# DLRM tower on one core: sixteen selected fields (two of them gathered in the middle units) and a 512- or 1024-word fill behind each gather, against twenty selected fields everywhere and three one-word fills

## The chip, the core and the metric

One NeuronCore of a Trainium2 chip runs the whole program. The time is device microseconds of one execution. Compute engines are PE (TensorE), DVE (VectorE), ACT (ScalarE) and POOL (GpSimd); SP (SyncE) only issues DMAs.

## The reference

2048 samples have 32 categorical fields each. Every field has a table with rows of 64 floats (26 tables have 1000 or 1250 rows, three 12500 and three 125000).

```python
e = jnp.stack([tbl_0[ids[:, 0]], ..., tbl_31[ids[:, 31]]], axis=1)   # 2048 x 32 x 64
gram = jnp.einsum('bnd,bmd->bnm', e, e)
z = gram[:, rows, cols]                       # 496 pairs, upper triangle
h = jnp.concatenate([z, dense_ctx], axis=1)   # 2048 x 512
h = jnp.maximum(h @ W_top1 + b_top1, 0.0)     # 512 -> 512
h = jnp.maximum(h @ W_top2 + b_top2, 0.0)     # 512 -> 256
y = h @ W_top3                                # 256 -> 1
```

All in float32.

## The kernel before, in words

The batch is cut into four units of 512 samples (`UNITS`, `UNIT`), and the samples of a unit into two rounds of 256 (`r`). A unit goes through four stages: its 32 embedding vectors per sample are fetched and laid into `vecs` (64 dims on partitions, twice, 256 samples x 32 fields on the free axis); the gram matrices are formed on PE from `vecs`; they go out to a DRAM scratch (`products`) and come back in another layout as `z`; the three layers of the tower run on `z`. The tower of a unit is woven into the gram stage of the next one, and that of the last unit stands alone at the end.

Fields are fetched in two ways.

*Selected* fields have small tables (1000 or 1250 rows, that is 8 or 10 chunks of 125 rows). The table lies in SBUF as three bfloat16 parts (`tabs`, PARTS = 3) whose sum is the float32 value; they are made in unit 0, on the way. Packed float32 chunks come by DMA into one of four stage slots (`load_stage`, SP). ACT copies the high part (`high`, L317), DVE subtracts it (`rest`, L436), ACT copies the middle part (`middle`, L322), DVE subtracts again (`low`, L441). For each chunk of 125 rows and 512 samples DVE makes a one-hot block (L453, `tensor_scalar` with `is_equal`, float16 ids broadcast to 128 partitions in `ids_wide`, 128x512), and PE multiplies each part of the chunk by it (L498, three matmuls for one one-hot). Fields go in pairs: one of a pair fills partitions 0 to 63 of `sel_ps`, the other 64 to 127. A pair is worked off in two halves, each of 4 or 5 chunks of both fields. `onehot` is a ring of four pieces (`RING`), a piece being one half of one field, so DVE can be two halves ahead of PE: it waits on `onehot_used` for the piece four back. PE waits on `onehot_ready` before each half. ACT empties `sel_ps` into `vecs` with four copies (L329, `selected`); there are two buffers.

*Gathered* fields come by indirect DMA from the tables in DRAM, issued by POOL (`gather`, L296): 128 rows of 256 bytes in one, so two (h) for each field and round. Behind each gather POOL fills a piece of `spare` with zeros (L303), a tile that nothing reads. Before the fill it waits until the fill before is done (`spaced`). The fill has 1024 words a partition in unit 0 and 512 in the others (`SPACING`). POOL then waits for nothing but `gat_full`: the slots in `rows` of a unit can be written over once PE has transposed those of the unit before. PE turns four fields at a time (`turn`, L513, four transposes into `gat_ps`, or two in the fifth turn of units 1 and 2), ACT copies them into `vecs` (`gathered`, L337).

Sixteen fields are selected in units 0 and 3 (eight pairs, 132 chunks: fourteen fields of 8 chunks and two of 10). In units 1 and 2 (`SHIFTED`) the last pair (fields 30 and 31, 10 chunks each) is gathered as well, which leaves seven pairs (112 chunks) and makes eighteen gathered fields.

The order of work is written by hand, one list for each engine. On PE a unit is: `select` of pairs 2 and up, with the turns of round 0 behind pairs 4, 5, ...; the turns that are left; layer 1 of the unit before in four pieces, each followed by a quarter of the gram matmuls of round 0 (L528); the turns of round 1, with `select` of pairs 0 and 1 of the next unit between them; layer 2, gram of round 1 and layer 3. ACT and DVE follow the same order. DVE in unit 0 does `one_hots`, `low`, `one_hots`, `rest` by turns, one pair after the other. ACT in unit 0 does `selected(g)`, `high(g+4)`, `middle(g+4)`. The gram stage of a unit starts when all its `selected` and `gathered` copies of round 0 are done.

SP issues all other DMAs in one list: the stage loads, `ids_wide` for each pair of the next unit (`load_wide`, each once DVE is done with the same pair of the unit before), then `products` out and `z` back.

## Time and profile before

| | |
|---|---|
| median of 3 runs | 574.52 us (572.3 to 587.05) |
| the profiled execution, its own time | 577.56 us |
| its span | 575.8 us |
| PE busy | 403.8 us (70%) |
| POOL busy | 465.0 us (81%) |
| DVE busy | 292.7 us (51%) |
| ACT busy | 141.8 us (25%) |
| granted TensorE clock, mean | 0.852 |

The span runs from the first to the last instruction of the profiled execution; 1.8 us of its own time lie around it. The granted clock is given as a share of full speed: 1.00 is 2.4 GHz, 0.50 is 1.2 GHz. The chain is the work that ended last, followed back from the end: what stands in it set the time. An instruction's duration in the trace runs from its start to its end, and consecutive ones of one engine overlap, so the pace is to be read from starts, or from the time of several divided by their count.

### The profile page before, as it was taken

The numbers are of one execution on the slowest core, as the hardware profiler recorded it, in microseconds if no ns is written. First come the engines' busy times: TensorE is split into PE (matmuls) and PEld (weight loads), VectorE is DVE, ScalarE is ACT, GpSimd is POOL, SyncE is SP. The second block draws the span as 40 slices with busy tenths as digits, with TensorE's granted clock in tenths as the row PEclk, the third lists the DMA queues.
The fourth block names the chain that finished last, engine by engine and source line by source line (L and its number), as shares of the span: only waits on it lengthen the run. The fifth ranks groups of instructions, "written<-read, shape, count | busy, mean of one in ns | idle before, by whom it ended". The sixth has DMA issues, their size and how long they took to land.

```text
span 575.8 us, 13498 instructions
## 1 busy us (share of the span) xinstructions
PE 403.8 (70%) x5956; PEld 217.7 (38%) x5956; DVE 292.7 (51%) x513; ACT 141.8 (25%) x232; POOL 465.0 (81%) x552
## 2 busy tenths in 40 slices
PE   0556554756874678787975687868966788799877
PEld 0222222323543334334432344334432344445655
DVE  4999999999180299300810499100900599100000
ACT  5002233422200334310201434111110434212212
POOL 7999999999998899989998999889988999950000
PEclk9977778787695699888986799887996799989989
DMA  8414311110111475110111584101011651003340
GB/s 271 140 51 141 98 33 32 30 35 15 21 21 23 73 166 150 29 23 20 22 21 23 101 190 124 23 21 21 21 23 23 132 119 19 19 16 64 72 83 1
DMA packets 39060, 36.11 MB, mean 63 GB/s; under 512 B 14869, under 2 KB 27991, under 8 KB 38874
## 3 DMA queue, kind: packets, MB, share of 16 engines
q1 hardware_dynamic: 29866, 25.14, 18.0%
q0 software_dynamic: 8704, 8.93, 7.6%
q8 instruction: 47, 0.77, 0.5%
q10 hardware_dynamic: 432, 1.18, 0.5%
q14 instruction: 11, 0.09, 0.0%
HBM read 27.15 MB, written 8.07 MB: 61 GB/s over the span
## 4 chain that ended last, share of the span: by engine, by line
PE 42%; DVE 39%; issue 11%; ACT 4%; DMA 2%; SPq 2%; ACTq 0%; DVEq 0%
DVE onehot L453 35%; PE gram_ps L528 14%; PE tower_ps L542 11%; PE sel_ps L498 9%; PE tower_ps L551 5%; ACT vecs L329 2%; PE tower_ps L560 2%; DVE work L436 2%; DVE tabs L441 2%; PE gat_ps L513 2%; DMA work<-in_packed_dram 1%; ACT work L346 1%; SPq L207 1%; DMA products<-work 1%; SPq L209 1%
## 5 line engine op out<-in xcount | busy, mean ns | idle before, releaser
L453 DVE TENSOR_SCALAR onehot<-ids_wide,row_ids 128x512 bf16<-128x512 f16 x488 | 269.4, 627 | 113.2 <-PE sel_ps L498 113.2
L296 POOL DMA_INDIRECT rows<-in_tbl_dram,gat_ids x272 | 287.0, 1055 | 46.3 <-issue 44.3
L498 PE MATMUL sel_ps<-onehot,tabs 128*64 128x512 bf16 x1464 | 200.4, 433 | 98.1 <-DVE onehot L453 79.5
L303 POOL MEMSET spare<- 128x512 f32 (+1 forms) x272 | 177.9, 654 | 0.1
L498 PEld LDWEIGHTS sel_ps<-onehot,tabs 128*64 128x64 bf16 x1464 | 95.9, 123 | 196.8 <-issue 95.2
L528 PE MATMUL gram_ps<-vecs 64*32 64x32 f32 x4096 | 71.2, 214 | 61.4 <-issue 48.8
L329 ACT COPY vecs<-sel_ps 64x256 f32<-64x256 f32 x120 | 71.9, 599 | 123.1 <-PE sel_ps L498 70.2
L528 PEld LDWEIGHTS gram_ps<-vecs 64*32 64x32 f32 x4096 | 54.6, 115 | 93.7 <-issue 80.5
L542 PE MATMUL tower_ps<-work,w_sb 128*128 128x512 f32 (+1 forms) x160 | 73.8, 622 | 2.8 <-DMA work<-products 2.8
L460 DVE COPY work<-gram_ps 128x512 f32<-128x512 f32 x8 | 5.2, 687 | 127.9 <-PE gram_ps L528 127.9
L542 PEld LDWEIGHTS tower_ps<-work,w_sb 128*128 128x128 f32 x160 | 35.7, 230 | 31.4 <-issue 25.3
L352 ACT ACTIVATE h<-tower_ps,b_sb 128x512 f32<-128x512 f32 (+1 forms) x20 | 12.0, 602 | 81.2 <-PE tower_ps L542 81.2
L551 PE MATMUL tower_ps<-h,w_sb 128*128 128x512 f32 (+1 forms) x80 | 31.0, 537 | 1.1 <-ACT h L352 1.1
L337 ACT COPY vecs<-gat_ps 128x512 f32<-128x512 f32 (+1 forms) x36 | 19.5, 570 | 34.8 <-PE gat_ps L513 29.5
L346 ACT COPY work<-gram_ps 128x512 f32<-128x512 f32 x24 | 13.0, 588 | 59.3 <-PE gram_ps L528 59.3
L322 ACT CAST tabs<-work 128x1024 bf16<-128x1024 f32 (+1 forms) x8 | 8.6, 1072 | 70.0 <-DVE work L436 70.0
L513 PE MATMUL gat_ps<-ident,rows 128*128 128x128 f32 x136 | 21.7, 293 | 4.9 <-ACT vecs L337 4.9
L513 PEld LDWEIGHTS gat_ps<-ident,rows 128*128 128x128 f32 x136 | 15.1, 145 | 14.4 <-issue 8.6
L551 PEld LDWEIGHTS tower_ps<-h,w_sb 128*128 128x128 f32 x80 | 15.1, 197 | 12.5 <-issue 9.7
L359 ACT ACTIVATE h<-tower_ps,b_sb 128x512 f32<-128x512 f32 (+1 forms) x10 | 5.5, 598 | 36.3 <-PE tower_ps L551 36.3
L560 PE MATMUL tower_ps<-h,w_sb 128*1 128x512 f32 (+1 forms) x20 | 11.1, 689 | 1.9 <-ACT h L359 1.9
L436 DVE TENSOR_TENSOR work<-work,tabs 128x1024 f32<-128x1024 f32 (+1 forms) x8 | 10.0, 1248 | 4.2 <-ACT tabs L317 4.2
(13 smaller groups left out, 25.1 us busy)
## 6 DMA issues: line engine op xcount, KB each, us to landing
ids_wide<-ids_scratch SPq DMA_DIRECT2D x30, 256.0 KB
rows<-in_tbl_dram,gat_ids POOLq DMA_INDIRECT x272
products<-work SPq DMA_DIRECT2D x12, 248.0 KB
products<-work SPq DMA_DIRECT2D x24, 120.0 KB
work<-in_packed_dram SPq DMA_DIRECT2D x5, 512.0 KB, 4.4
work<-products SPq DMA_DIRECT2D x9, 256.0 KB
work<-in_packed_dram ACTq DMA_DIRECT2D x2, 512.0 KB, 6.1
w_sb<-in_w_dram SPq DMA_DIRECT2D x1, 1024.0 KB
```

The source lines that it names most:

```text
L296: nc.gpsimd.indirect_dma_start(out=rows[:, r, k, h, :], out_offset=None, in_=tables[ROWS_OF[k]], in_offset=bass.IndirectOffsetOnAxis(ap=ga ...
L303: nc.gpsimd.memset(spare[:, 0:SPACING[u]], 0.0).then_inc(spaced, 1)
L329: last = nc.scalar.copy(vecs[DIM * h:DIM * h + DIM, :, N_GAT + 2 * g + at], sel_ps[DIM * at:DIM * at + DIM, sel_no(u, g) % 2, HALF * h:HAL ...
L337: nc.scalar.copy(vecs[:, P * r:P * r + P, at], gat_ps[:, n % 2, 0:P * fields].rearrange("p (f j) -> p j f", f=fields))\
L436: nc.vector.tensor_tensor(piece, piece, tabs[:, c0:c0 + k, 0, :], ALU.subtract).then_inc(rest_ready, 1)
L453: last = nc.vector.tensor_scalar(onehot[:, n % RING, c - c0, :], ids_wide[:, k, :], row_ids[chunks[k]][:, c:c + 1], None, ALU.is_equal)
L498: last[at] = nc.tensor.matmul(sel_ps[DIM * at:DIM * at + DIM, n % 2, :], tabs[:, first_chunk[k] + c, part, :], onehot[:, piece_no(u, g, ha ...
L513: last = nc.tensor.transpose(gat_ps[:, n % 2, P * at:P * at + P], rows[:, r, k, :, :].rearrange("p h d -> p (h d)"), ident[:])
L528: last = nc.tensor.matmul(gram_ps[32 * s:32 * s + 32, h, i, :], v, v, start=True, stop=True, skip_group_check=True)
L542: last = nc.tensor.matmul(tower_ps[:, j % 2, 0:width], w1_sb[:, c, P * j:P * j + P], z[:, c, x0:x0 + width], start=(c == 0), stop=(c == Q ...
L551: last = nc.tensor.matmul(tower_ps[:, o, 0:width], w2_sb[:, j, P * o:P * o + P], h1[:, j, 0:width], start=(j == 0), stop=(j == J1 - 1), sk ...
L560: last = nc.tensor.matmul(tower_ps[0:1, 0, 0:width], w3_sb[:, o:o + 1], h2[:, o, 0:width], start=(o == 0), stop=(o == J2 - 1))
```

## The change

Fields 16, 21, 23 and 29 (1250 rows, 10 chunks each) are selected as well, in front of 30 and 31. All units are alike: twenty selected fields in ten pairs (seven pairs of 16 chunks and three of 20, 172 in all), and twelve gathered fields in three turns of four. `SHIFTED`, the fifth turn and the functions that counted uneven units go. `tabs` grows by four fields, and unit 0 has two more stage loads and two more `high`, `rest`, `middle` and `low`. In place of the fill of 1024 or 512 words there are three fills of one word behind each gather, each waiting for the one before.

```diff
-SELECTED = [7, 8, 9, 11, 12, 15, 17, 18, 20, 22, 24, 25, 27, 28, 30, 31]
+SELECTED = [7, 8, 9, 11, 12, 15, 17, 18, 20, 22, 24, 25, 27, 28, 16, 21, 23, 29, 30, 31]
...
-SHIFTED = (1, 2)
-ROWS_OF = GATHERED + SELECTED[-2:]
-N_ROWS = len(ROWS_OF)
-ALL_PAIRS, ALL_TURNS = N_SEL // 2, N_GAT // 4 + 1
+GROUPS = [range(k, min(k + 4, N_GAT)) for k in range(0, N_GAT, 4)]
+N_PAIRS, N_TURNS = N_SEL // 2, len(GROUPS)
...
-SPACING = [1024, 512, 512, 512]
-PAIRS = [ALL_PAIRS - (u in SHIFTED) for u in range(UNITS)]
-TURNS = [ALL_TURNS - (u not in SHIFTED) for u in range(UNITS)]
+SPACERS = 3
...
             def gather(u, r, x):
-                for v in [v for v in range(u) if x < TURNS[v]][-1:]:
-                    pool.wait_ge(gat_full, gat_no(v, r, x) + 1)
-                for k in range(N_ROWS)[turn_slots(x)]:
+                if u > 0:
+                    pool.wait_ge(gat_full, gat_no(u - 1, r, x) + 1)
+                for k in GROUPS[x]:
...
-                        spaced_no = next(count)
-                        if spaced_no > 0:
-                            pool.wait_ge(spaced, spaced_no)
-                        nc.gpsimd.memset(spare[:, 0:SPACING[u]], 0.0).then_inc(spaced, 1)
+                        for _ in range(SPACERS):
+                            n = next(count)
+                            if n > 0:
+                                pool.wait_ge(spaced, n)
+                            nc.gpsimd.memset(spare[:], 0.0).then_inc(spaced, 1)
...
             for u in range(UNITS):
-                for g in range(2, PAIRS[u]):
+                for g in range(2, N_PAIRS):
                     select(u, g)
-                    if g >= 4:
-                        turn(u, 0, g - 4)
-                for x in range(PAIRS[u] - 4, TURNS[u]):
-                    turn(u, 0, x)
+                    if g >= N_PAIRS - N_TURNS:
+                        turn(u, 0, g - N_PAIRS + N_TURNS)
```

PE in unit 0, from its first matmul to the gram matmuls of round 0. L498 and after the change L468 are the matmuls by one-hots, L513 and L482 the transposes of gathered rows, L528 and L497 the gram. Before:

```order
L498 MATMUL sel_ps<-onehot,tabs 64x512 x240
L513 MATMUL gat_ps<-ident,rows 128x128 x4
L498 MATMUL sel_ps<-onehot,tabs 64x512 x48
L513 MATMUL gat_ps<-ident,rows 128x128 x4
L498 MATMUL sel_ps<-onehot,tabs 64x512 x48
L513 MATMUL gat_ps<-ident,rows 128x128 x4
L498 MATMUL sel_ps<-onehot,tabs 64x512 x60
L513 MATMUL gat_ps<-ident,rows 128x128 x4
L528 MATMUL gram_ps<-vecs 32x32 x256
L513 MATMUL gat_ps<-ident,rows 128x128 x8
```

After:

```order
L468 MATMUL sel_ps<-onehot,tabs 64x512 x396
L482 MATMUL gat_ps<-ident,rows 128x128 x4
L468 MATMUL sel_ps<-onehot,tabs 64x512 x60
L482 MATMUL gat_ps<-ident,rows 128x128 x4
L468 MATMUL sel_ps<-onehot,tabs 64x512 x60
L482 MATMUL gat_ps<-ident,rows 128x128 x4
L497 MATMUL gram_ps<-vecs 32x32 x256
L482 MATMUL gat_ps<-ident,rows 128x128 x8
```

The first turn now stands behind eight pairs (396 matmuls) in place of five (240), and unit 0 has 516 matmuls by one-hots where it had 396.

PE in unit 1, from the gram matmuls of unit 0's round 1 to layer 1 of unit 0 (L542, after the change L511). Before:

```order
L528 MATMUL gram_ps<-vecs 32x32 x256
L498 MATMUL sel_ps<-onehot,tabs 64x512 x144
L513 MATMUL gat_ps<-ident,rows 128x128 x4
L498 MATMUL sel_ps<-onehot,tabs 64x512 x48
L513 MATMUL gat_ps<-ident,rows 128x128 x4
L498 MATMUL sel_ps<-onehot,tabs 64x512 x48
L513 MATMUL gat_ps<-ident,rows 128x128 x10
L542 MATMUL tower_ps<-work,w_sb 128x512 x4
L528 MATMUL gram_ps<-vecs 32x32 x64
```

After:

```order
L497 MATMUL gram_ps<-vecs 32x32 x256
L468 MATMUL sel_ps<-onehot,tabs 64x512 x300
L482 MATMUL gat_ps<-ident,rows 128x128 x4
L468 MATMUL sel_ps<-onehot,tabs 64x512 x60
L482 MATMUL gat_ps<-ident,rows 128x128 x4
L468 MATMUL sel_ps<-onehot,tabs 64x512 x60
L482 MATMUL gat_ps<-ident,rows 128x128 x4
L511 MATMUL tower_ps<-work,w_sb 128x512 x4
L497 MATMUL gram_ps<-vecs 32x32 x64
```

Between the two gram stages stand 420 matmuls by one-hots where 240 stood, and three turns of four where there were turns of 18 transposes in all; behind the last `select` comes one turn of four in place of ten transposes.

DVE at the end of unit 0. L453 and L423 are the one-hots, L436 and L406 `rest`, L441 and L411 `low`, L460 and L430 copies of gram results. Before:

```order
L436 TENSOR_TENSOR work<-work,tabs 128x1280
L453 TENSOR_SCALAR onehot<-ids_wide,row_ids 128x512 x8
L441 TENSOR_TENSOR tabs<-work,tabs 128x20x64
L453 TENSOR_SCALAR onehot<-ids_wide,row_ids 128x512 x76
L460 COPY work<-gram_ps 128x32x16 x2
L453 TENSOR_SCALAR onehot<-ids_wide,row_ids 128x512 x112
```

After:

```order
L406 TENSOR_TENSOR work<-work,tabs 128x1280
L423 TENSOR_SCALAR onehot<-ids_wide,row_ids 128x512 x10
L411 TENSOR_TENSOR tabs<-work,tabs 128x20x64
L423 TENSOR_SCALAR onehot<-ids_wide,row_ids 128x512 x10
L406 TENSOR_TENSOR work<-work,tabs 128x1280
L423 TENSOR_SCALAR onehot<-ids_wide,row_ids 128x512 x10
L411 TENSOR_TENSOR tabs<-work,tabs 128x20x64
L423 TENSOR_SCALAR onehot<-ids_wide,row_ids 128x512 x78
L430 COPY work<-gram_ps 128x32x16 x2
```

Two more pairs have their `rest` and `low` between the one-hots. Of those behind the last `low`, 28 of 76 belonged to unit 0 and 30 of 78 do now; the other 48 are pairs 0 to 2 of unit 1.

## Rows read from the trace of the kernel before

**Rows 1.** Busy time of each engine, and the granted clock in 40 slices.

```profile
PE 403.8 (70%) x5956; PEld 217.7 (38%) x5956; DVE 292.7 (51%) x513; ACT 141.8 (25%) x232; POOL 465.0 (81%) x552
PEclk9977778787695699888986799887996799989989
```

**Rows 2.** The chain that ended last, shares of the span by engine.

```profile
PE 42%; DVE 39%; issue 11%; ACT 4%; DMA 2%; SPq 2%; ACTq 0%; DVEq 0%
```

**Rows 3.** Busy time by stretch: the selecting stretches of units 0 to 3.

```profile
12.40:130.00 117.60, 66.86 (x378) 30.58 (x378) 117.60 (x147) 31.12 (x43) 109.66 (x97) 0.80 0.25 72
194.90:231.30 36.40, 30.43 (x249) 15.55 (x250) 31.92 (x71) 13.28 (x23) 33.15 (x42) 0.96 0.67 153
...
448.40:495.20 46.80, 39.04 (x313) 19.81 (x314) 37.89 (x84) 16.17 (x27) 42.56 (x54) 0.94 0.42 83
```

**Rows 4.** The chain in order of time, unit 1: start, duration, what.

```profile
194.94 4.38 PE sel_ps L498 x24
...
199.38 6.66 DVE onehot L453 x15
...
228.43 2.83 PE sel_ps L498 x24
...
233.71 0.59 ACT vecs L337
...
234.79 5.13 PE tower_ps L542 x8
239.92 0.70 PE gram_ps L528 x49
```

**Rows 5.** The chain in order of time, unit 3's selecting.

```profile
448.37 5.38 PE sel_ps L498 x24
...
482.59 9.12 DVE onehot L453 x20
...
491.75 3.43 PE sel_ps L498 x30
495.18 0.59 PE gat_ps L513 x4
495.77 3.44 PE tower_ps L542 x8
```

**Rows 6.** The one-hots alone by stretch: length, DVE busy (count), granted clock, DMA.

```profile
199.40:228.10 28.70, 28.70 (x64) 1.00 0.68 162
...
12.40:130.00 117.60, 103.40 (x133) 0.80 0.25 72
```

**Rows 7.** Instructions in time, unit 0: start, duration, engine, operation; narrow windows.

```profile
14.56 0.34 DVE L453 TENSOR_SCALAR onehot<-ids_wide,row_ids 128x512 bf16<-128x512 f16 x1
14.82 1.75 DVE L453 TENSOR_SCALAR onehot<-ids_wide,row_ids 128x512 bf16<-128x512 f16 x1
...
15.46 0.96 POOL L303 MEMSET spare<- 128x1024 f32 x1
16.59 1.06 POOL L296 DMA_INDIRECT rows<-in_tbl_dram,gat_ids  x1 [0.17 <-issue]
```

**Rows 8.** The same around 330 us, unit 2.

```profile
329.62 1.07 POOL L296 DMA_INDIRECT rows<-in_tbl_dram,gat_ids  x1 [0.16 <-issue]
330.69 0.58 POOL L303 MEMSET spare<- 128x512 f32 x1
331.42 1.07 POOL L296 DMA_INDIRECT rows<-in_tbl_dram,gat_ids  x1 [0.16 <-issue]
...
329.79 1.02 DVE L453 TENSOR_SCALAR onehot<-ids_wide,row_ids 128x512 bf16<-128x512 f16 x2
330.73 0.69 DVE L453 TENSOR_SCALAR onehot<-ids_wide,row_ids 128x512 bf16<-128x512 f16 x1
```

**Rows 9.** A one-word fill of POOL at the start of the program.

```profile
0.31 0.10 POOL L654 MEMSET const-bfloat16-1.0<- 128x1 bf16 x1
```

**Rows 10.** The groups of instructions, shapes apart: `rest` of the pair of 20 chunks.

```profile
L436 DVE TENSOR_TENSOR work<-work,tabs 128x1280 f32<-128x1280 f32 x1 | 1.5, 1472 | 0.0
```

**Rows 11.** PE in unit 0: the first half pair, and the last on the chain.

```profile
18.92 5.29 PE L498 MATMUL sel_ps<-onehot,tabs 128*64 128x512 bf16 x24 [18.92 <-DVE onehot L453]
...
130.01 5.07 PE sel_ps L498 x29
```

**Rows 12.** The chain in order of time, pairs 0 and 1 of unit 2.

```profile
275.75 6.42 DVE onehot L453 x14
```

**Rows 13.** POOL's gathers by stretch: length, POOL busy (count), clock, DMA.

```profile
157.80:512.70 354.90, 205.60 (x207) 0.86 0.27 58
```

More of the change, by code:

```diff
@@ L86, in piece_no @@
 def piece_no(u, g, half, at):
-    return 4 * (PAIRS_TO[u] + g) + 2 * half + at
+    return 4 * (N_PAIRS * u + g) + 2 * half + at
 def pair_row(n, m):
@@ L99, in dlrm_tower_kernel @@
     half_most = max(b - a for h in halves for a, b in h)
-    pair_chunks = [(first_chunk[2 * g], chunks[2 * g] + chunks[2 * g + 1]) for g in range(ALL_PAIRS)]
+    pair_chunks = [(first_chunk[2 * g], chunks[2 * g] + chunks[2 * g + 1]) for g in range(N_PAIRS)]
     pair_most = max(k for _, k in pair_chunks)
-    assert all(chunks[2 * g] == chunks[2 * g + 1] for g in range(ALL_PAIRS))
+    assert all(chunks[2 * g] == chunks[2 * g + 1] for g in range(N_PAIRS))
     with ExitStack() as ctx:
@@ L165, in dlrm_tower_kernel @@
         spaced = sem("spaced")
-        rows_in = [[sem(f"rows_in{r}_{x}") for x in range(ALL_TURNS)] for r in range(ROUNDS)]
+        rows_in = [[sem(f"rows_in{r}_{x}") for x in range(N_TURNS)] for r in range(ROUNDS)]
         sel_emptied = sem("sel_emptied")
@@ L193, in load_wide @@
             def load_wide(u, w):
-                last = [v for v in range(u) if w < PAIRS[v]][-1:]
-                for v in last:
-                    sp.wait_ge(onehot_ready, piece_no(v, w, 1, 1) + 1)
+                if u > 0:
+                    sp.wait_ge(onehot_ready, piece_no(u - 1, w, 1, 1) + 1)
                 sp.dma_start(ids_wide[:, WIDE * w:WIDE * w + WIDE, :],
@@ L246, in _ @@
                 load_wide(0, w)
-            for g in range(STAGE_SLOTS, MOST_PAIRS):
+            for g in range(STAGE_SLOTS, N_PAIRS):
                 load_stage(g)
@@ L254, in _ @@
             for u in range(LAST):
-                for w in range(PAIRS[u + 1]):
+                for w in range(N_PAIRS):
                     load_wide(u + 1, w)
@@ L308, in _ @@
                 for r in range(ROUNDS):
-                    for x in range(TURNS[u]):
+                    for x in range(N_TURNS):
                         gather(u, r, x)
@@ L405, in _ @@
                 gram(u, 0, 1, (0, 1))
-                for x in range(TURNS[u]):
+                for x in range(N_TURNS):
                     gathered(u, 1, x)
@@ L445, in one_hots @@
                 if half == 0:
[L446 removed]
+                    dve.wait_ge(wide_in[g], 16 * (u + 1))
                 for at in range(2):
@@ L465, in _ @@
             rest(1)
-            for g in range(MOST_PAIRS):
+            for g in range(N_PAIRS):
                 one_hots(0, g, 0)
-                if g + 1 < MOST_PAIRS:
+                if g + 1 < N_PAIRS:
                     low(g + 1)
                 one_hots(0, g, 1)
-                if g + 2 < MOST_PAIRS:
+                if g + 2 < N_PAIRS:
                     rest(g + 2)
             for u in range(1, UNITS):
-                for g in range(PAIRS[u]):
+                for g in range(N_PAIRS):
                     one_hots(u, g, 0)
@@ L586, in _ @@
                     select(u + 1, 1)
-                for x in range(3, TURNS[u]):
+                for x in range(3, N_TURNS):
                     turn(u, 1, x)
```

60 lines of the change are left out of this document (23 added, 37 removed).

## The prediction

> **What bounds the kernel now.** I read the shares of busy time first, then the chain that ended last, then the chain in order of time around the borders of the units, then the busy times by stretch, and last single instructions of DVE and POOL side by side. The reader is to see that no engine is busy all the time: POOL has 81%, PE 70%, DVE 51% [rows 1]. The chain is shared by PE (42%) and DVE (39%) [rows 2], one after the other. While fields are selected DVE is on it, making one-hots; in the gram and tower stages PE is. In unit 0's selecting stretch DVE is busy for all 117.6 us and PE for 66.9 of them [rows 3]. In unit 1 the chain holds 15 or 16 one-hots in 6.7 us again and again, between a first half pair on PE of 4.4 us and a last one of 2.8 us [rows 4]. POOL, though the busiest, is in no part of the chain.
>
> So the pace of a one-hot matters. It is 103.4 us / 133 = 0.78 us in unit 0 and 28.7 / 64 = 0.45 us in unit 1 [rows 6], for the same instruction. Single instructions show why. Undisturbed, one starts 0.26 us behind the other (14.56, 14.82) [rows 7]. The one that starts at 14.82 then lasts 1.75 us in place of 0.34 and ends 0.15 us after the 1024-word fill; three one-hots go by in a POOL cycle of 2.20 us. With the 512-word fill four go by in a cycle of 1.80 us: one is held 0.4 us by the gather (two take 1.02 us in place of 0.6), one 0.35 us by the fill of 0.58 us (0.69 in place of 0.34) [rows 8]. PE needs three matmuls for a one-hot: 2.83 us / 8 = 0.354 [rows 4] or 3.43 / 10 = 0.343 at the full clock [rows 5], so 0.347, and 5.29 / 8 = 0.66 at the half clock [rows 11]. DVE at 0.45 is slower than PE at the full clock, so it bounds; at 0.26 it would be faster, and PE would.
>
> The Trainium skill, in "SBUF — State Buffer", section "SBUF: two separate sides", calls the port pair that the two engines share an exclusive lock, held for a whole instruction by whichever starts first. The fill rows agree. The gather rows don't: a one-hot that starts at 329.79 ends inside the gather of 329.62 to 330.69 [rows 8], so only a part of a gather shuts DVE out.
>
> **The change, part by part.** The sum is made against the profiled execution: 575.8 us of span and 1.8 around it, 577.6; the median shown is 574.5, 3 us less.
>
> *The fills.* No row shows three one-word fills with waits between. One such fill lasts 0.10 us alone [rows 9]. A POOL cycle is then a gather of 1.07 and the gap of 0.16 [rows 8], 0.3 of fills and two waits of 0.05 to 0.25 us: 1.6 to 2.0, say 1.65. If the fills hold DVE for nothing, it loses 0.42 of 1.65 and makes 1.23 / 0.26 = 4.7 one-hots: 0.35 each. If each holds it for its 0.10, 0.93 / 0.26 = 3.6, so 0.46. I take 0.40, in between; the nearest row is 0.45, with the 512-word fill. The bounds by rows are 0.26, as if nothing disturbed it, and 0.78, as with the long fill. In unit 0 the old pace was 1.06 times what its cycle alone gives (2.20 / 3 = 0.73), so 0.42 there.
>
> *Unit 0.* One-hots go from 132 to 172, and two more pairs need `rest` and `low`: four instructions at some 1.4 us (1.47 alone [rows 10]), 5.6 us. DVE's other work was 117.6 - 103.4 = 14.2 us. New: 14.2 + 5.6 + 172 x 0.42 = 92.0 us in place of 117.6, 25.6 less. But PE, with 516 matmuls, needs 0.66 for a one-hot at the half clock and is then behind DVE. The clock in this stretch is 0.80 on average [rows 3]. I give back 2.6 us for it: **-23**. ACT's two more pairs of casts and copies hide behind DVE, and so do two more stage loads and `ids_wide` loads on SP (DMA share 0.25 [rows 3]); the last load is asked for three and a half pairs, some 30 us, before it is needed.
>
> *Units 1 and 2.* One-hots between the gram stages go from 80 to 140. POOL has 48 gathers a unit, 48 x 1.65 = 79 us, freed by the turns of the unit before, so most of them run beside the gram stage. Before, they ran without a break, 207 in 355 us [rows 13]. Through most of the selecting stretch POOL should be idle, DVE at 0.26, and PE bounds: the first half pair at the half clock 4.4 [rows 4], then 132 x 0.347 = 45.8. The turns behind pairs 7 and 8 set off new gathers, which puts the last 40 one-hots at 0.40: 2.1 more. 52.3 us against 36.3 (194.9 to 231.3): **+16 each, +32**.
>
> *Unit 3.* Selecting took 448.4 to 495.2, 46.8. Now 5.4 for the first half pair [rows 5] + 45.8 = 51.2, no gathers behind it: **+4.4**.
>
> *Fewer turns.* In units 1 and 2 PE ended selecting at 231.26 and could start layer 1 at 234.79 only, since the fourth and fifth turn waited for ACT's copies (the chain goes through ACT up to 233.71 + 0.59 [rows 4]). With one turn behind the last pair, as in unit 3, it is 0.6 us [rows 5]: 2.9 saved twice, **-5.8**. Of the 40 transposes that go, 20 lie on PE's path outside this and outside DVE's time; four take 0.59 us [rows 5]: **-3**. *Pairs 0 and 1 of the next unit* in the gram stage were paced by DVE (14 one-hots in 6.42 [rows 12]); at 0.40 for 0.45 it is 0.5 us twice: **-1**.
>
> *Fewer gathers.* 272 to 192, and POOL was in no wait of the chain: nothing.
>
> Sum: -23 + 32 + 4.4 - 5.8 - 3 - 1 = +3.6. That gives 581.2 against the profiled execution and 578 against the median; I say 580. The change takes DVE off the path after unit 0 and puts as much PE work on it: saved where DVE bounds, paid where PE does. After it PE is next: 403.8 + 600 x 0.116 to 0.22 us, less 6, is 467 or more.
>
> **The rivals.**
> 1. *PE at the half clock through unit 0.* If the clock stays at 1.2 GHz there, PE takes 172 x 0.66 = 113.5 us from 18.9 [rows 11], to 132.4; its last matmul was at 135.1. Unit 0 gives 3 us, not 23: 601 us, **slower**. For it: the clock was 0.7 in five slices of that stretch [rows 1], with PE busy 66.9 of 117.6 us [rows 3]. Against it: at 0.42 DVE feeds PE more densely, and at PE busy for 30.4 of 36.4 us the clock was 0.96 [rows 3]. It decides from the point where PE spends over half of unit 0 at 1.2 GHz.
> 2. *The short fills shut DVE out too*, one-hots at 0.46, 0.48 in unit 0: 10 us of unit 0's gain go and 5 more in units 1 and 2, 596 us, **slower**. It needs 0.1 us held for each fill. For it: the fill of 0.58 us did hold a one-hot 0.35 [rows 8]. The skill's lock rule, above, is this rival; by it the sum would be 596.
> 3. *The fills are nearly free and the cycle is longer.* With waits that stretch it to 2.0 us DVE has 1.58 of 2.0 and makes a one-hot each 0.33; at 0.32 to 0.33 unit 0 takes 76 us, 42 less, and PE at the full clock keeps up (172 x 0.347 = 60): 562 us, **faster**.
> 4. *DVE doesn't get its 0.26 in the selecting stretches* (gathers still run there, or 0.26 holds for only a few in a row), pace 0.45 there as well: units 1 and 2 take 4.4 + 132 x 0.45 + 2.8 = 66.6, 14 more each, unit 3 16 more, rival 2 on top: 636 us. For it: no row shows over three undisturbed one-hots in a row. Against it: the sizes of POOL's work above.
>
> **How the numbers follow.** Forecast 0.50, rivals 0.15, 0.15, 0.13 and 0.07. What a measurement can tell from no change is some 2%, 11.5 us, so 563 to 586. The forecast lies within, with a little of its spread above; rivals 1, 2 and 4 are slower, rival 3 is faster: faster 0.12, within 0.51, slower 0.37. The range takes in rivals 1, 2 and 3 and leaves out the fourth: 559 to 603. The forecast's own is 571 to 591.
>
> **What would show it.** Unit 0's last one-hot at 105 us (at 119 or more: rival 1 or 2; at 90: rival 3). One-hots in unit 0 at 0.42. POOL idle for most of 180 to 210 us and one-hots started 0.26 us apart where PE lets them; PE busy without a break and DVE waiting on it in the selecting stretches of units 1 to 3, 52 us long. The gap between selecting and layer 1 at 0.6 us. The forecast is wrong if the chain still goes through one-hots in units 1 to 3, or if PE waits for gathered rows.

## The result, and the profile after

The changed kernel took 567.24 us (median of 5 runs, 566.95 to 568.54) beside 573.26 us for the kernel before (5 runs): ratio 0.9904, 95% interval 0.9877 to 0.9931. That is 1% faster: clear of no change by the interval, though less than the 2% that the prediction called no change. The forecast was 580 us, 1% slower. Where one of a kernel's runs lay over 1.5% above its fastest, it is left out of the medians below; so e10, e11 and e17 stand with one run each. Nearly every stage moved, by up to 48 us. In the profiled executions (575.8 and 566.7 us of span), cut at the first and last matmul of `select`:

| stage | before | after | moved | forecast |
|---|---|---|---|---|
| unit 0, to the end of selecting | 135.0 | 87.3 | -47.7 | -23 |
| unit 0, two gram stages | 46.6 | 77.7 | +31.1 | 0 |
| unit 0, pairs 0 and 1 of unit 1 between them | 13.3 | 12.6 | -0.7 | |
| unit 1, selecting | 36.3 | 49.9 | +13.6 | +16 |
| unit 2, selecting | 36.0 | 47.6 | +11.6 | +16 |
| unit 3, selecting | 46.8 | 49.2 | +2.4 | +4.4 |
| units 1 and 2, four gram stages with tower layers | 153.9 | 147.3 | -6.6 | -8.8, with turns and transposes |
| units 1 and 2, pairs 0 and 1 between | 27.3 | 22.5 | -4.8 | -1 |
| the rest, from unit 3's gram stages | 80.6 | 72.6 | -8.0 | |

The page of the changed kernel (busy times, granted clock by slice, the gram matmuls, the chain by engine; they answer to [rows 1, 2]), and its busy times by stretch, for [rows 3]:

```profile
PE 444.4 (78%) x6516; PEld 252.2 (45%) x6516; DVE 224.8 (40%) x717; ACT 166.3 (29%) x264; POOL 265.1 (47%) x776
PEclk9999996557755999869967999969966799999989
L497 PE MATMUL gram_ps<-vecs 64*32 64x32 f32 x4096 | 85.5, 218 | 79.6 <-issue 67.8
PE 65%; issue 11%; DVE 10%; another core or an unknown queue 6%; ACT 4%; DMA 2%; SPq 2%; ACTq 0%; DVEq 0%
```

```profile
core 0: us, PE busy (x) PEld busy (x) DVE busy (x) ACT busy (x) POOL busy (x), PEclk, DMA share, GB/s
17.30:87.30 70.00, 58.52 (x515) 29.69 (x512) 67.40 (x183) 38.71 (x52) 61.68 (x158) 1.00 0.43 134
87.30:131.90 44.60, 19.71 (x528) 13.73 (x526) 2.30 (x8) 5.68 (x10) 31.91 (x101) 0.53 0.10 20
177.60:227.50 49.90, 49.55 (x429) 27.86 (x429) 36.88 (x132) 20.67 (x34) 11.78 (x33) 0.95 0.52 119
```

DVE's part came out as planned, or better: it fell from 39% of the chain to 10%, and PE is busy for 49.55 of 49.90 us while unit 1 selects. The second stretch is the surprise. Between selecting and the next selecting PE is busy for 19.7 of 44.6 us, and beside it only POOL does much (31.9 us). The chain there, and single instructions of it:

```profile
89.83 0.59 ACT vecs L309
90.42 32.87 another core or an unknown queue
123.37 1.08 ACT work L318 x2
```

```profile
99.73 0.34 PE L497 MATMUL gram_ps<-vecs 64*32 64x32 f32 x5 [0.41 <-issue]
99.87 0.94 POOL L267 DMA_INDIRECT rows<-in_tbl_dram,gat_ids  x1
100.49 0.21 PEld L497 LDWEIGHTS gram_ps<-vecs 64*32 64x32 f32 x6 [0.56 <-issue]
100.50 0.34 PE L497 MATMUL gram_ps<-vecs 64*32 64x32 f32 x5 [0.42 <-issue]
100.81 0.43 POOL L275 MEMSET spare<- 128x1 f32 x3
101.23 0.34 PE L497 MATMUL gram_ps<-vecs 64*32 64x32 f32 x5 [0.40 <-issue]
101.39 0.94 POOL L267 DMA_INDIRECT rows<-in_tbl_dram,gat_ids  x1
```

"Another core or an unknown queue" is a wait whose releaser the chain didn't find: ACT waits for `gram_full`, so for PE. PE waits for no semaphore. It issues five matmuls, stops for 0.4 us ("issue": nothing in the profile explains it), issues five more, two bursts for each POOL cycle of 1.52 us. The 256 matmuls of the first half gram stage (`b` = 0 of one round) take from 90.6 to 119.5 us, with 19 gathers beside them. A half with POOL idle takes 2.2 us at the full clock, as in unit 3, and 4.7 at the half clock that was granted in this stage (e3, below). I call PE "held" where it goes like this, and "free" where it doesn't. The kernel before was held too, less hard, and not in its first gram stage (halves of 5.9 and 5.2 us with three gathers each, for 4.7 and 5.7 without any in e3). Its page has 61.4 us of idle PE ahead of these matmuls, 48.8 of it "issue", a row that stood in none of my groups:

```profile
L528 PE MATMUL gram_ps<-vecs 64*32 64x32 f32 x4096 | 71.2, 214 | 61.4 <-issue 48.8
```

### The profile page after: what moved, and what is told of

It is laid out like the page before. It is cut to its first block, busy times and chain, and to the rows that moved or that the text cites. A ratio compares the mean times of both kernels' runs of the same rounds, so it can differ in the third digit from the quotient of the medians.

```text
span 566.7 us, 15098 instructions
## 1 busy us (share of the span) xinstructions
PE 444.4 (78%) x6516; PEld 252.2 (45%) x6516; DVE 224.8 (40%) x717; ACT 166.3 (29%) x264; POOL 265.1 (47%) x776
## 4 chain that ended last, share of the span: by engine, by line
PE 65%; issue 11%; DVE 10%; another core or an unknown queue 6%; ACT 4%; DMA 2%; SPq 2%; ACTq 0%; DVEq 0%
PE sel_ps L468 33%; PE gram_ps L497 12%; PE tower_ps L511 11%; DVE onehot L423 7%; PE tower_ps L520 5%; PE gat_ps L482 2%; ACT vecs L301 2%; DVE tabs L411 2%; PE tower_ps L529 2%; DVE work L406 1%; DMA work<-in_packed_dram 1%; ACT work L318 1%; DMA products<-work 1%; SPq L180 0%
## 5 line engine op out<-in xcount | busy, mean ns | idle before, releaser
L468 PE MATMUL sel_ps<-onehot,tabs 128*64 128x512 bf16 x2064 | 236.3, 388 | 34.5 <-ACT vecs L301 16.9
L423 DVE TENSOR_SCALAR onehot<-ids_wide,row_ids 128x512 bf16<-128x512 f16 x688 | 196.2, 358 | 166.2 <-PE sel_ps L468 164.9
L267 POOL DMA_INDIRECT rows<-in_tbl_dram,gat_ids x192 | 191.5, 998 | 146.1 <-PE gat_ps L482 119.8
L468 PEld LDWEIGHTS sel_ps<-onehot,tabs 128*64 128x64 bf16 x2064 | 126.5, 112 | 138.6 <-issue 35.6
L497 PE MATMUL gram_ps<-vecs 64*32 64x32 f32 x4096 | 85.5, 218 | 79.6 <-issue 67.8
L301 ACT COPY vecs<-sel_ps 64x256 f32<-64x256 f32 x160 | 96.9, 606 | 100.0 <-PE sel_ps L468 92.0
L497 PEld LDWEIGHTS gram_ps<-vecs 64*32 64x32 f32 x4096 | 63.2, 118 | 116.5 <-issue 103.6
L275 POOL MEMSET spare<- 128x1 f32 x576 | 73.3, 127 | 22.1
L511 PE MATMUL tower_ps<-work,w_sb 128*128 128x512 f32 (+1 forms) x160 | 68.4, 584 | 2.7 <-DMA work<-products 2.2
L430 DVE COPY work<-gram_ps 128x512 f32<-128x512 f32 x8 | 5.2, 687 | 134.3 <-PE gram_ps L497 134.3
L511 PEld LDWEIGHTS tower_ps<-work,w_sb 128*128 128x128 f32 x160 | 34.2, 221 | 27.3 <-issue 21.7
L294 ACT CAST tabs<-work 128x1024 bf16<-128x1024 f32 (+1 forms) x10 | 11.1, 1109 | 27.3 <-DVE work L406 21.1
L309 ACT COPY vecs<-gat_ps 128x512 f32<-128x512 f32 x24 | 13.8, 592 | 17.2 <-PE gat_ps L482 16.9
L482 PE MATMUL gat_ps<-ident,rows 128*128 128x128 f32 x96 | 15.7, 297 | 0.6 <-ACT vecs L309 0.6
L406 DVE TENSOR_TENSOR work<-work,tabs 128x1024 f32<-128x1024 f32 (+1 forms) x10 | 13.0, 1295 | 3.8 <-ACT tabs L289 3.8
L482 PEld LDWEIGHTS gat_ps<-ident,rows 128*128 128x128 f32 x96 | 10.8, 147 | 7.2 <-issue 6.2
L411 DVE TENSOR_TENSOR tabs<-work,tabs 128x1024 bf16<-128x1024 f32 (+1 forms) x10 | 12.9, 1292 | 1.2 <-ACT tabs L294 1.2
```

The costliest lines, as they stand in the source:

```text
L267: nc.gpsimd.indirect_dma_start(out=rows[:, r, k, h, :], out_offset=None, in_=tables[GATHERED[k]], in_offset=bass.IndirectOffsetOnAxis(ap=g ...
L275: nc.gpsimd.memset(spare[:], 0.0).then_inc(spaced, 1)
L301: last = nc.scalar.copy(vecs[DIM * h:DIM * h + DIM, :, N_GAT + 2 * g + at], sel_ps[DIM * at:DIM * at + DIM, sel_no(u, g) % 2, HALF * h:HAL ...
L406: nc.vector.tensor_tensor(piece, piece, tabs[:, c0:c0 + k, 0, :], ALU.subtract).then_inc(rest_ready, 1)
L411: nc.vector.tensor_tensor(tabs[:, c0:c0 + k, 2, :], stage[g % STAGE_SLOTS][:, 0:k, :], tabs[:, c0:c0 + k, 1, :], ALU.subtract).then_inc(ta ...
L423: last = nc.vector.tensor_scalar(onehot[:, n % RING, c - c0, :], ids_wide[:, k, :], row_ids[chunks[k]][:, c:c + 1], None, ALU.is_equal)
```

## The experiments

Ratios are to runs of the kernel before that stood beside the experiment. Four chips were used: e1 to e4, e17 and e18 ran on one (A), e5 to e8 on B, e9 to e12 on C, e13 to e16 on D. That of the first measurement is not on record. On A the kernel before took 563.8 to 572.8 us. On B, C and D its runs fall into two groups, 555 to 558 us and 566 to 571 us, and the ratios there are to the lower one.

### The two halves of the change

**e1**, the fields alone, with the long fills:

```diff
-SPACERS = 3
+SPACERS = 1
+SPACING = [1024, 512, 512, 512]
...
-                            nc.gpsimd.memset(spare[:], 0.0).then_inc(spaced, 1)
+                            nc.gpsimd.memset(spare[:, 0:SPACING[u]], 0.0).then_inc(spaced, 1)
```

> The changed kernel with the old fills (one of 1024 words in unit 0, of 512 after it) in place of three of one word: the fields alone. Theory A (each gather that POOL issues beside the gram matmuls stops PE's stream of short matmuls for some 1.3 us, and the fill only sets how many gathers fall into a gram stage): one-hots of unit 0 at 0.78 us again, so selecting ends near 170 us in place of 87; half a gram stage (128 products, from its first to its last matmul) takes 8 to 10 us beside the 512-word fills in place of 15 to 29; about 600 us. Theory B (the three short fills with their waits do it, not the gathers): half a gram stage at 2 to 5 us, 560 to 580 us. Theory C (PE is slow there because its clock is at 1.2 GHz): the gram stages stay as long as now, 640 us.

**e2**, the fills alone: the kernel before with three one-word fills.

```diff
+                        for _ in range(3):
...
-                        nc.gpsimd.memset(spare[:, 0:SPACING[u]], 0.0).then_inc(spaced, 1)
+                            nc.gpsimd.memset(spare[:, 0:1], 0.0).then_inc(spaced, 1)
```

> The kernel before with three one-word fills behind each gather in place of the long one: the fills alone. Theory A: one-hots of unit 0 at 0.29 us, so its selecting stretch ends near 72 us in place of 135; half gram stages at 15 to 29 us in place of 5 to 10, some 60 us more over the kernel; 555 to 590 us. Theory B: the same. Theory C: gram stages as before, so 510 us.

Measured: e1 583.2 us, ratio 1.0287 [1.0219, 1.0355]; e2 578.47 us, 1.0194 [1.0139, 1.0249]. Each half alone makes the kernel slower; together they made it 1% faster in the first measurement. In e1 unit 0 selects until 137.3 us (135.0 in the first profile of the kernel before, 123.4 in its second, e17), not until 170, and most half gram stages beside gathers stay at 6 to 10 us, as theory A had it. Theory C, the clock alone, had 640 and 510 us and falls with both runs. In e2 it selects until 70.7 us, 64 us earlier than before, and all of it is lost again: halves of 10 to 20 us, and 97.0 us of "issue" ahead of the gram matmuls for 48.8. Theory B had the same for e2, so e2 doesn't part it from A.

### Gathers or fills?

**e3** runs POOL's list for unit 0 alone; **e4** keeps all fills but issues gathers in unit 0 only. In both PE waits for the rows of unit 0 only, and units 1 to 3 compute with those.

```diff
-            for u in range(UNITS):
+            for u in range(1):
```

> The changed kernel without the gathers and fills of units 1 to 3: PE transposes the rows of unit 0 again, so those units compute with unit 0's rows for the twelve gathered fields. Theory A: every half gram stage takes 2.2 to 4.6 us (2.2 is what is seen with POOL idle at the full clock), which takes 104 us off: about 463 us. Theory B: the same 463. Theory C: 567.

```diff
+                        if u == 0:
...
                             nc.gpsimd.indirect_dma_start(
```

> As the run without gathers after unit 0, but POOL keeps the three one-word fills with their waits in units 1 to 3, 48 times three a unit; only the gathers are left out. Theory A: as without them, about 463 us. Theory B: gram stages as slow as in the changed kernel, 540 to 567 us. Theory C: 567.

e3: 453.64 us, 0.7992 [0.7942, 0.8041]. e4: 455.41 us, 0.8023 [0.7971, 0.8074]. These stood beside e1 and e2 on one chip. Their gram matmuls on the pages (e3, then e4):

```profile
L497 PE MATMUL gram_ps<-vecs 64*32 64x32 f32 x4096 | 44.0, 209 | 21.1 <-issue 12.9
```

```profile
L498 PE MATMUL gram_ps<-vecs 64*32 64x32 f32 x4096 | 44.3, 210 | 20.6 <-issue 12.4
```

The idle time goes with the gathers; the fills with their semaphores, kept in e4, don't bring it back. e4 is 123 us below e2, on the same chip, and 112 below the changed kernel's first measurement, for gathers that are in no part of the chain before.

### Four runs that seemed to prove a remedy

**e5** lets POOL start the gathers of a unit's second turn only when the gram matmuls of round 0 of the unit before are done, and those of the turns after it only when round 1's are; **e6** adds one fill for three in units 1 to 3; **e7** fetches plain rows by SP's queue and **e8** by POOL's in units 1 to 3 (so the contents are others).

```diff
                     pool.wait_ge(gat_full, gat_no(u - 1, r, x) + 1)
+                    if (r, x) == (0, 1):
+                        pool.wait_ge(gram_full, emptied_no(u - 1, 1, 0))
+                    elif (r, x) != (0, 0):
+                        pool.wait_ge(gram_full, emptied_no(u, 0, 0))
```

> The changed kernel with the gathers kept off the gram stages: of the gathers for a unit the first turn's may run as now, the second's only once the gram matmuls of round 0 of the unit before are done, all others only once those of round 1 are. Same instructions otherwise. Theory A (a gather beside gram matmuls holds PE some 1.3 us, beside selecting nothing, as one-hots at 0.29 us stay under PE's 0.347): half gram stages of units 0 to 3 at 2.2 to 5 us but for the few gathers that spill over; 465 to 485 us. A rival, that the cost only moves (PE's selecting matmuls are held too): 550 us or more.

```diff
-                        for _ in range(SPACERS):
+                        for _ in range(SPACERS if u == 0 else 1):
```

> As the run before it, with one one-word fill behind a gather in units 1 to 3 in place of three. Theory A: the cycle falls from 1.55 to some 1.3 us, so fewer gathers spill from the selecting stretch into the gram stage: 3 to 12 us less than with three fills, unless the one-hots get slower than 0.347 us, which would cost up to 5 us a unit.

```diff
+                        for k in GROUPS[x]:
+                            for h in range(2):
+                                sp.dma_start(rows[:, r, k, h, :], ...
```

> The changed kernel with the gathers of units 1 to 3 replaced by plain transfers of the same shape (128 rows of 256 bytes, 2 KB apart in the table, so not the rows that the ids name) that SP issues, behind the same turns and so beside the same gram stages; POOL is idle then. Theory A1 (what holds PE is POOL issuing a transfer in software): half gram stages at 2.2 to 5 us, 453 to 470 us. Theory A2 (what holds it is the transfer of 128 short rows itself): half gram stages at 10 us or more, 540 us or more.

```diff
+                        else:
+                            nc.gpsimd.dma_start(rows[:, r, k, h, :], ...
```

> The same plain transfers, issued by POOL where the gathers of units 1 to 3 stood, with their three fills. If anything that POOL issues in software holds PE: half gram stages as in the changed kernel, 15 us and more, 540 to 570 us. If only the indirect form does (ids read, one descriptor for each row): 453 to 480 us.

Measured: e5 458.77 us (0.8242 [0.8153, 0.8331]), e6 458.66 (0.8274 [0.816, 0.8388]), e7 451.74 (0.8134), e8 454.4 (0.8182). I read this as: gathers moved beside the selecting matmuls cost nothing, and only the indirect form holds PE. Neither follows: the changed kernel was not run beside them, and e13 shows that it can be free itself.

### What POOL's rhythm does

**e9** has no fills (`SPACERS = 0`), **e12** one one-word fill in units 1 to 3 (e6's edit), both without e5's waits. **e10** is e5 with one fill of 1024 words in unit 0:

```diff
-                        for _ in range(SPACERS):
+                        for _ in range(1 if u == 0 else SPACERS):
...
-                            nc.gpsimd.memset(spare[:], 0.0).then_inc(spaced, 1)
+                            nc.gpsimd.memset(spare[:, 0:1024 if u == 0 else 1], 0.0).then_inc(spaced, 1)
```

**e11** is the kernel before with POOL's list for unit 0 alone.

> The changed kernel without any fill behind a gather, gathers not held back. Theory 'each gather costs': a gather that runs beside the short matmuls of a gram stage costs them 0.9 to 1.4 us whatever follows it on POOL. The gathers then stand closer (cycle 1.0 to 1.1 us for 1.5), so the first half of the first gram stage, with some 16 to 20 gathers in it, takes 18 to 24 us for 29.0, and the total is 545 to 565 us. Theory 'fills hold PE' (already weak): the halves fall to 2.2 to 4 us each and the total is near 460. In unit 0 the run also asks who holds DVE: if it is the gather, one-hots with gathers close together are slower than the changed kernel's 0.29 us (0.42 lost per 1.05 us of cycle gives 0.43, and selecting ends near 110 us); if it was the fill, they are at 0.26 to 0.30 and selecting ends at 85 to 90 us.

> The kernel of run e5 (gathers held back until the first gram round of the unit has been through PE) with one fill of 1024 words behind each gather in unit 0 and three of one word later. It prices the short fills in unit 0 by themselves, with the gram stages of the later units the same. The fills' theory: unit 0's selecting ends at 135 to 140 us for 87, and the total is 458.8 + 48 to 53 = 506 to 512 us. Rival (the clock of PE, not the fill, sets unit 0's pace): selecting ends before 110 us and the total is under 485.

> The kernel before with the gathers of unit 0 alone; those of units 1 to 3 are left out, with the fills behind them. It asks how much the gathers held the kernel before, and prices the change of fields without them. Theory 'each gather costs': the half gram stages fall from 5 to 11 us to 2.2 to 4.6, 13 halves by some 5.5 us = 70; one-hots of units 1 and 2 are no longer held either, 80 at 0.347 for 0.45 = 8 us each: total 566.8 - 70 - 16 = 480, range 470 to 495. Rival (gathers held only the changed kernel, the ones before had other limits): over 530.

> The changed kernel with one one-word fill behind each gather of units 1 to 3 in place of three, gathers not held back. Theory 'each gather costs': a shorter POOL cycle (about 1.25 us for 1.5) puts the same gathers into the same gram stages and shortens each half by the share of the fills: halves of 22 to 26 us for 29.0 and a total of 550 to 568 us. Theory 'fills or their semaphores cost': two of three fills less takes two thirds of the loss off, halves near 10 us, total under 510.

Measured: e9 468.34 us (0.8378 [0.8263, 0.8493]), e10 502.3, e11 454.0, e12 464.5 (0.8336 [0.8254, 0.8418]). My theory of a fixed 0.9 to 1.4 us for each gather fell as a rule for every run: in e9 and e12 gathers come every 1.25 us beside the same matmuls, and a half takes 2.7 to 6 us with two to seven of them. In e9 the one-hots of unit 0 took 0.31 us and selecting ended at 92.0 us, nearer to what I expected if the fill held DVE than to the 0.43 and 110 us for the gather. e10 comes near its forecast of 506 to 512: 502.3 - 458.8 = 43.5 us for the long fill of unit 0, where selecting ends at 133.7 us for 87.1 in e5. e11 is 103 us below the kernel before beside it (557.3), 26 lower than I expected: without the gathers of units 1 to 3 and the fills behind them, the kernel before loses its time on chip C too.

### The control, and what it overturned

> The changed kernel, unchanged. A control: runs e9 and e12 fell to 468 and 464 us though their gathers were not held back, so it must be known that the changed kernel still takes 567 us beside them. Both theories below: 563 to 572 us, half gram stages of 15 to 29 us. If it comes out near 460, the loss is one of occasion and not of the kernel.

**e14** puts `pool.wait_ge(ident_zero, 1)`, long met, where e5 waits for `gram_full`.

> The changed kernel with a wait at each place where run e5 held POOL back, but on a condition long met, so that POOL's rhythm and the order of all work stay. Theory 'rhythm': a gather holds PE's short matmuls for long only where POOL comes round slowly (1.5 us and more, with the gathers running on through the gram stage), and for 0.1 to 0.6 us at 1.25 us a cycle: nothing changes, 560 to 572 us. Rival 'placement': any small change of POOL's instructions shifts something and the loss goes away: near 460 us, and e5 then proved nothing about holding gathers back.

**e15** is the kernel before with `SPACING[u] if u == 0 else 1` words; **e16** the changed kernel with one fill of 512 words in units 1 to 3.

> The kernel before, with the one fill behind each gather of units 1 to 3 cut from 512 words to one; unit 0 keeps 1024. Theory 'rhythm': POOL's cycle goes from 1.65 to 1.25 us, the half gram stages of units 1 and 2 from 7.4 to 9 to 3 to 4 us, those of unit 0's second round likewise, 12 halves by some 4 to 5 us and 80 one-hots twice a little faster: 567 - 50 to 70 = 495 to 515 us. Rival (the 24-field split or the number of turns keeps it slow): over 545 us.

> The changed kernel with one fill of 512 words behind each gather of units 1 to 3 in place of three of one word. It keeps one fill, as e12 (464.5 us), but a cycle of 1.65 us, as the kernel before. Theory 'rhythm': half gram stages of 7 to 12 us and a total of 515 to 575 us. Rival 'number of fills and waits' (one is harmless, three are not): near 465 to 475 us.

Measured: e13, the changed kernel, 465.14 us (463.23 and 467.05) where its first measurement gave 567.2; e14 459.93, e15 461.84, e16 483.49; the kernel before 556.8 to 570.1 beside them. e13's instructions are those of the first profile, in the same order on every engine. Its stretches:

```profile
17.30:87.20 69.90, 58.21 (x515) 29.44 (x511) 67.58 (x183) 38.70 (x52) 61.60 (x158) 1.00 0.45 138
87.20:104.80 17.60, 9.79 (x526) 8.27 (x524) 2.30 (x8) 5.34 (x10) 14.32 (x45) 0.57 0.12 24
131.70:183.00 51.30, 50.43 (x429) 27.41 (x429) 38.58 (x132) 20.64 (x34) 41.73 (x117) 0.94 0.55 130
```

Unit 0's selecting agrees to 0.1 us. The gram stage behind it takes 17.6 us for 44.6, at a granted clock of 0.57 for 0.53, so the clock isn't it. And POOL has the same rhythm beside the same matmuls (single instructions of e13):

```profile
90.54 2.89 PE L497 MATMUL gram_ps<-vecs 64*32 64x32 f32 x194
90.72 0.94 POOL L267 DMA_INDIRECT rows<-in_tbl_dram,gat_ids  x1
91.66 0.42 POOL L275 MEMSET spare<- 128x1 f32 x3
92.23 0.94 POOL L267 DMA_INDIRECT rows<-in_tbl_dram,gat_ids  x1
```

194 matmuls go by in 2.9 us, in and between gathers 1.51 us apart, where the first profile let ten through in 1.52. Over the program, the six gaps between selecting stretches in units 0 to 2 take 118.1 us here and 224.9 there: 106.8 us, all of the difference (566.7 - 461.4 = 105.3). Not all of it is idle time: PE is busy for 444.4 us there and for 398.5 here. Unit 1's first gram stage shows why, in the first profile and in e13:

```profile
227.50:266.20 38.70, 30.66 (x560) 16.26 (x558) 2.44 (x8) 7.76 (x13) 20.23 (x65) 0.78 0.08 16
183.00:204.90 21.90, 21.74 (x560) 12.19 (x558) 2.44 (x8) 7.18 (x12) 17.39 (x54) 1.00 0.11 23
```

Held, PE idles between short bursts and the granted clock falls to the half in between, so that the tower matmuls woven in are slower as well: eight of them take 6.6 us from 241.4 us on, at a clock of 0.55, for 3.7. Over units 1 and 2 the tower layers take 61.8 us for 50.2.

So one program has two times, and which it shows is a matter of the occasion or the chip. e14 says nothing more than e13, and e5 to e9 no longer show a remedy. "Rhythm" is refuted as the cause by e13 (1.52 us, free) and e16 (one 512-word fill, free).

**e17** is the kernel before, **e18** is e2 again, both profiled on chip A.

> The kernel before, unchanged, with a profile of its own beside the later runs. The changed kernel has shown two times, 567.2 us (first measurement) and 465.1 (run e13), with the same instructions in the same order, and half gram stages of 15 to 29 us in the one and 2.6 to 5.4 in the other. Theory 'two modes of the machine, and in every run the kernel before has been in the held one or has no other': span 553 to 570 us, half gram stages of 5 to 10 us in units 1 and 2 as in its first profile. If its halves are 2.6 to 5 us here and its span is still over 550, its time lies somewhere else than in the gram stages and the table by stage will say where.

> Run e2 once more (the kernel before with three one-word fills for the long one; 24 selected fields, 272 gathers), which took 578.5 us with half gram stages of 10 to 20 us. If the mode belongs to the occasion, as it did for the changed kernel, PE is not held: half stages of 3 to 6 us, unit 0's selecting ends at 70 us as then, and the total is run e15's 461.8 less the 53 us that unit 0 gains = 405 to 420 us. That would make it the fastest version, and the change of fields a loss of some 50 us where gathers don't hold PE. If it belongs to the kernel (272 gathers at 1.52 us a cycle), it is 570 to 585 us again.

Measured: e17 563.8 us, span 562.0, halves of 7 to 10.5 us from unit 0's second round to the last with gathers beside it; e18 578.48 us, ratio 1.0143 [1.0071, 1.0214], as e2. Both held. e18's first half gram stage, all its gram matmuls, and the chain:

```profile
74.20:94.70 20.50, 10.19 (x256) 6.70 (x256) 0.00 (x0) 0.00 (x0) 0.51 0.12 24
```

```profile
PE 55%; another core or an unknown queue 16%; issue 12%; DVE 9%; ACT 5%; DMA 2%; SPq 2%; ACTq 0%; DVEq 0%
L529 PE MATMUL gram_ps<-vecs 64*32 64x32 f32 x4096 | 108.4, 219 | 114.5 <-issue 95.9
```

and e17's gram matmuls, for the row of the kernel before above:

```profile
L528 PE MATMUL gram_ps<-vecs 64*32 64x32 f32 x4096 | 70.3, 213 | 62.4 <-issue 52.6
```

What stays open: what decides between held and free. Every profile with gathers beside gram matmuls on chip A was held (e1, e2, e17, e18), every one on B, C and D was free (e5, e6, e9, e10, e12 to e16). The chip alone would explain that, but not the kernel before, which kept its 555 to 571 us on B, C and D. Free, it should take some 481 us (an estimate: e15's 461.8 and the 19 us by which e16's 512-word fill exceeds e12). It was not profiled there.

That it was held there too is therefore argued, not shown. For it speak its mean granted clock, 0.83 to 0.87 in all its runs as in its two held profiles (0.852 and 0.869), where e15, free, has 0.907; and e11. If so, the chip doesn't decide alone: on D the step from 512 words to one after unit 0 takes the kernel before from 556.8 to 461.8 us, and the changed kernel only from 483.5 (e16) to e13's 465.1.

Within the held profiles my theory fits: in units 1 to 3 of before, after, e17 and e18 each gather beside a half adds 1.0 to 1.4 us to the 2.2 without any; in e13 and e15 it adds 0.2 to 0.4. Nor was e2's kernel, or one with gathers held back as in e5, run free and held both.

## Why the prediction was wrong

Two steps failed. The size of unit 0's term, -23, was wrong: it measured -47.7, since a one-hot took 0.29 us and not 0.42. And "Fewer gathers: nothing" was wrong in its mechanism: gathers beside the gram stages hold PE, which cost 31.1 us in unit 0. The two misses nearly cancel, and smaller ones turned the sign (the sum, below).

**Unit 0 (the term -23; measured -47.7).** The mechanism was right, its size wrong: the pace. I took 0.42 us for a one-hot, from three short fills that hold DVE for part of their 0.10 us and a gather that costs it 0.42 in each cycle. The rows that answer to [rows 6, 7], of the changed kernel up to 90 us and at 26 us:

```profile
L423 DVE TENSOR_SCALAR onehot<-ids_wide,row_ids 128x512 bf16<-128x512 f16 x188 | 55.3, 364 | 2.6 <-PE sel_ps L468 2.6
```

```profile
26.21 2.32 DVE L423 TENSOR_SCALAR onehot<-ids_wide,row_ids 128x512 bf16<-128x512 f16 x8
```

55.3 / 188 = 0.29. POOL's cycle is 1.71 us there (I had 1.65), in which 5.8 one-hots go by, so gather and fills together cost DVE 1.71 - 5.8 x 0.26 = 0.2 us and not over 0.42: the gather's share was too large as well as the fills'. That is rival 3 (nearly free fills, PE at full clock behind them), which put the stretch at -42 and had 0.13. The last one-hot of unit 0 ended at 83.2 us; I had named 105 for the forecast and 90 for rival 3. Rival 1 fell: the clock was 1.00 over the stretch. Rival 2 fell with the reading of the Trainium skill ("SBUF — State Buffer", section "SBUF: two separate sides") by which each fill, short or not, shuts DVE out for its whole time. Long fills do hold DVE: with the 512-word fill the one-hots of unit 1 take 0.42 a piece in e16 for 0.29 in e12 (mean durations overlap; pace is 56.1 / 133 and 39.4 / 134), and the selecting stretch 61.8 us for 50.8.

```profile
L423 DVE TENSOR_SCALAR onehot<-ids_wide,row_ids 128x512 bf16<-128x512 f16 x133 | 56.1, 499 | 7.6 <-PE sel_ps L468 7.6
```

```profile
L423 DVE TENSOR_SCALAR onehot<-ids_wide,row_ids 128x512 bf16<-128x512 f16 x134 | 39.4, 369 | 13.2 <-PE sel_ps L468 13.2
```

Not all of the -47.7 belongs to the fills. In the first profile of the kernel before, DVE and POOL ran in step: from 18.8 to 108.6 us every third gather started 0.09 us behind a `rest` or `low` and took 1.94 or 2.20 us in place of 1.06. In e17, the same program, the gather beside each `rest` and `low` starts 0.16 us ahead of it and takes 1.06 us, and selecting ends at 123.4 us, 11.6 earlier. Single instructions of both, two lines each:

```profile
93.28 1.20 DVE L441 TENSOR_TENSOR tabs<-work,tabs 128x1024 bf16<-128x1024 f32 x1
93.37 1.94 POOL L296 DMA_INDIRECT rows<-in_tbl_dram,gat_ids  x1 [0.17 <-issue]
```

```profile
63.52 1.06 POOL L296 DMA_INDIRECT rows<-in_tbl_dram,gat_ids  x1 [0.17 <-issue]
63.69 1.21 DVE L436 TENSOR_TENSOR work<-work,tabs 128x1024 f32<-128x1024 f32 x1
```

A one-hot of unit 0 takes 92.2 / 133 = 0.69 us in e17 for 0.78, so the factor of 1.06 that the prediction took over from the old pace belonged to this step, and against e17 unit 0's selecting gains 36.1 us and not 47.7. The 1% hangs on it too: e17's span (562.0) is below the changed kernel's (566.7).

**Selecting in units 1 to 3 (+16, +16, +4.4; measured +13.6, +11.6, +2.4).** Right in kind. DVE made one-hots 0.27 apart, waited for PE, and PE was busy without a break; I had let each first half pair run at the half clock, which it did in unit 1 (5.0 us at a clock of 0.52) and for 3.4 us in unit 3 (0.55), but not in unit 2 (1.00). After it unit 1 takes 44.9 us for its 132 one-hots, 0.340 each for my 0.347, and the 2.1 us for the last 40 were not needed.

```profile
185.37 2.19 DVE L423 TENSOR_SCALAR onehot<-ids_wide,row_ids 128x512 bf16<-128x512 f16 x8 [0.33 <-PE sel_ps L468]
```

**Turns (-5.8).** Right: the gap between selecting and layer 1 is 0.4 us in units 1 and 2 (in unit 1 selecting ends at 227.54 and layer 1 starts at 227.96), for 3.5.

**"Fewer gathers: nothing", and no term for the gram stages.** This is the step whose mechanism failed. POOL was in no wait of the chain, and from that I took that its gathers cost PE nothing. In unit 0 the gram stages gained 31.1 us against me, since 37 gathers fell into their halves in place of 19, and those of the first half added 1.3 us each where none of the first stage had added more than 0.4; with the short fills alone (e18) they gained still more. In units 1 and 2 this ate part of what turns and transposes gave (-6.6 for -8.8). In unit 3 it paid: no gathers are left beside its gram stages, its first half takes 2.2 us for 7.0 there, and the rest of the program is 8.0 us shorter. e3 and e4 show whose time it is where PE is held: without gathers beside the gram stages its idle time goes. That such a loss comes and goes between runs of one program (e13) no row of before could tell, and its cause stays open.

**The sum.** Moved: -47.7 + 31.1 - 0.7 + 13.6 + 11.6 + 2.4 - 6.6 - 4.8 - 8.0 = -9.1 us, as the spans have it. Forecast: +3.6. Two misses, of -24.7 in unit 0's selecting and +31.1 behind it, nearly cancelled; the smaller ones add up to -19.1 (selecting in units 1 to 3 -8.8, the end -8.0, the rest -2.3), and with the +6.4 that the two leave make the 12.7 us between +3.6 and -9.1. So the smaller ones turned the sign, and that the time lies in the range (559 to 603) is luck: without the 31.1 us that the prediction lacked it would have been some 536 us. The forecast's own 571 to 591 assumed that PE's share behind selecting stood still.

**What the change is worth when PE is free.** The first measurement compares two held kernels. Beside it, e10 and e16 price the short fills at 43.5 us (unit 0) and 19 (the others). The fields cost some 40: e15 (sixteen selected, 1024 words in unit 0, one later) has 461.8 and e10 (twenty selected, 1024 words, three of one later) 502.3. That is rough, since e10 also holds its gathers back; the selecting stretches of units 1 to 3 alone take 30.0, 29.8 and 37.3 us for 49.9, 48.4 and 48.8. So the fills are the good half and the fields the bad one, the signs of my steps. Sixteen selected fields with short fills throughout should be the best of all, 461.8 - 43.5 = some 418 us free, an estimate that no run shows: e18 was to show it and was held. The fastest complete versions run were e6 and e5, 458.7 and 458.8 us, below the kernel before beside them; but only 6 us below the changed kernel's 465.1 in e13, on another chip.

## What to carry to other kernels

An idle row with "issue" as its cause, on the engine that the chain names most, is a term of the sum: ask which engine is active during it and what the change does to that engine's rhythm there. Making one stage shorter moves what ran beside it into the next; follow each background stream past the border. And before a chain of experiments, run the kernel under study itself once beside the first of them, on the same chip: here a control beside e5 would have told a remedy from an occasion on which PE was free anyway.

## What the runs showed of the hardware

- Indirect gathers issued by POOL can hold PE's short matmuls (64 rows, 32 columns, with a weight load each): bursts of five every 0.76 us, 29.0 us for 256 matmuls with 19 gathers beside them, at a granted clock of 0.50; without gathers 4.7 us at that clock and 2.2 at 1.00 (e3). On another occasion (e13) the same half of the same program took 5.0 us, with four gathers in it. It isn't the clock: in unit 1 of the kernel before PE is held at a granted clock of 1.00 too (8.2 us for a half).
- A held PE can lose its clock as well: 0.78 over unit 1's first gram stage, held, for 1.00 free, and the tower matmuls in it take up to 6.6 us for 3.7.
- Held, the word that PE is done comes late as well: in the changed kernel the last matmul of the first half ends at 119.75 us, its increment stands in the trace at 123.28 and ACT starts at 123.37. In the kernel before ACT starts 1.3 to 1.5 us after the last matmul beside gathers and 0.04 to 0.10 us without; in e13, free, 0.03 to 0.6 us.
- The long matmuls of selecting (512 columns) were not held by gathers in any run: in the changed kernel's first profile, where PE is held in the gram stages, 60 of them take 6.67 us with four gathers beside them (unit 2) and 6.67 without (unit 3); in e13 117 POOL instructions run beside them and PE is busy for 50.43 of 51.30 us.
- Three one-word fills behind a gather take 0.43 us, cost DVE almost nothing, and even help: without any, one-hots of unit 0 are at 59.0 / 188 = 0.31 us in e9 for 0.29, since gathers come every 1.25 us.
- A gather that starts 0.09 us behind a `tensor_tensor` of DVE (1.2 us) takes 1.94 us; one that starts 0.16 us ahead of it takes 1.06, as without. In the kernel before the two engines can stay in such a step for 90 us.
